# Who splits the expert weights: ScalarE and GpSimd alone, VectorE no more

## The chip, the core and the metric

The kernel runs on one core of a Trainium2 chip. Its engines are TensorE (PE, matrix products), VectorE (DVE), ScalarE (ACT), GpSimd (POOL) and SyncE (SP, which issues transfers). The metric is the device time of one launch in microseconds, the median of several runs; less is better.

## What is computed

The input is 4 sequences of 1024 rows of 256 numbers in fp32. A layer norm, an RMS norm, a projection to q, kv and a gate, a gated scan along the sequence and a residual come first. Then comes a mixture of experts, which takes most of the time:

```python
logits = x_flat @ router_w.T                      # 4096 rows, 7 experts
top_vals, top_idx = jax.lax.top_k(logits, 2)
top_w = jax.nn.softmax(top_vals, axis=-1)
g = jnp.einsum('nd,edh->enh', x_flat, wg)         # 256 -> 1024
u = jnp.einsum('nd,edh->enh', x_flat, wu)
out = jnp.einsum('enh,ehd->end', silu(g) * u, wd) # 1024 -> 256
```

The two chosen experts of a row are weighted and added, a shared expert and the residual are added too. The result is needed at fp32 accuracy.

## The kernel before

**Products in three terms.** TensorE multiplies fp32r numbers here. Each fp32 operand is split into a rounded part `hi` and a remainder `lo = value - hi`, and a product is hi\*hi + hi\*lo + lo\*hi. So each weight, each row block `xs` and each hidden block `h` has to be split before it is used.

**Slots.** The rows of the experts are worked off in slots of 256 rows: 8 slots of the shared expert (numbers 0 to 7), 38 routed slots (8 to 45, rows sorted by expert through DRAM), 8 shared slots again (46 to 53). `SA` is 8, `ROUTED` 38, `NB0` 46. A slot has 96 products for gate and up (`ps<-xs_..,w_..`, L731), in 4 pairs of 24, and 48 for down (L748), in 4 quarters of 12. TensorE may begin pair p + 2 only when VectorE has taken pair p out of PSUM (semaphore `gated`), and quarter p of down only when `h_lo` of pair p is there (`h_ready`).

**Work on a pair.** ScalarE makes `silu` (L546) from PSUM. VectorE makes `h` = PSUM \* silu (L1031). ScalarE rounds it to `h_hi` (L551). VectorE makes `h_lo` = h - h_hi (L1041), with both inputs in SBUF. Once in a slot the next rows are turned (`turn_x`, L875), rounded (`x_hi`, L490) and their remainder made (`x_lo`, L881, one input in PSUM).

**Weights.** In each routed slot a new set of weights is used, three parts of 128x2048: gate (k = 0), up (k = 1), down (k = 2). There are two buffers of `w_hi` and `w_lo`, and one `raw` for each part. SyncE loads a part into `raw` once its last remainder is made (`wlo_ready`). In slot n the set of slot n + 1 is prepared: VectorE casts gate after pair 0 and up after pair 1 (`split_hi`, L1011) and makes up's remainder in two halves after pairs 2 and 3 (`split_lo`, L1017). ScalarE casts down at the slot's end (L559). GpSimd makes the remainders of gate and down (L423, 128x2048 each, both inputs in SBUF).

**Order.** Each engine works off its own program in the order in which it is written; semaphores are the only ties between engines. An instruction that waits holds up all behind it on its engine.

Of the kernel before, what the change touches and what calls it, by code (L numbers as in the profile page):

```python
# [21 lines left out]
def preln_scan_moe_kernel(nc, x, w_qkva, gamma, router_w, w_gate, w_up, w_down,  # L22
# [12 lines left out]
    ST = SLOT // P  # L35
# [33 lines left out]
    with ExitStack() as ctx:  # L69
# [172 lines left out]
        PARTS = (2, 1, 0)  # L242
        PART_BANKS = (0, 1, 6)
        WARM = 18
        POOL_LO = (0, 2)
        NB0 = SA + ROUTED

        def place_of(j, p):
# [14 lines left out]
        def _(sp):  # L263
# [47 lines left out]
                        load_x(u, u, z_dram, u)  # L311

            def load_w(sources, m):
                for k, src in enumerate(sources):
                    sp.wait_ge(wlo_ready[k], m)
                    sp.dma_start(raw_v[k], src).then_inc(raw_in[k], 16)
# [51 lines left out]
        def _(pool):  # L368
# [72 lines left out]
            for t in range(TILES):  # L441
                for k in range(TOP):
                    pool.indirect_dma_start(  # L443
                        sorted_dram, bass.IndirectOffsetOnAxis(ap=pos[:, k, t:t + 1], axis=0),
                        z_all[:, t, :], None, bounds_check=ROUTED * SLOT - 1).then_inc(scat, 16)
            for k in POOL_LO:
                split_lo(k, 1, 1)
            with pool.Fori(0, ROUTED // 2) as i:
                for u in range(2):
                    for k in POOL_LO:  # L450
                        split_lo(k, i * 2 + (u + 2), u)


            for u in range(2):
                pool.wait_ge(y_out[u], 16 + 16 * (ROUTED // 2))
# [13 lines left out]
        def _(act):  # L469
# [70 lines left out]
            def slot(n, u, r=None, m=None, load=None, last=False, between=()):  # L540

                for p in range(PAIRS):
                    q = n * PAIRS + p
                    par = p % 2
                    act.wait_ge(gu_psum, q + 1)
                    act.activation(silu[:, par, :, :], ps[:, 2 * par:2 * par + 2, 0:SLOT], ACT.Silu  # L546
                                   ).then_inc(silu_ready, 1)
                    act.wait_ge(gated, q + 3)
                    if p == 0:
                        act.wait_ge(down_psum, n + 1)  # L550
                    act.activation(h_hi[:, 2 * p:2 * p + 2, :], h32[:, par, :, :], ACT.Copy  # L551
                                   ).then_inc(hhi_ready, 1)
                    if p in between:
                        between[p]()
                if not last:
                    x_hi(n + 1, 1 - u)
                if m is not None:
                    act.wait_ge(raw_in[2], load)
                    act.activation(w_hi[u][:, 2, :], raw[:, 2, :], ACT.Copy).then_inc(whi_ready[2], 1)  # L559
                if r is not None:  # L560
                    act.wait_ge(down_psum, n + 2)
                    act.wait_ge(y_out[u], r)
                    act.activation(y_rows[:, u, :, :], ps[:, 4:6, 0:D], ACT.Copy
                                   ).then_inc(down_free, 1)
                    act.wait_ge(down_free, n + 2)
                    act.dma_start(rows_of(y_dram, n - SA), y_rows[:, u, :, :]).then_inc(y_out[u], 16)
# [12 lines left out]
            slot(SA - 1, 1, m=1, load=32)  # L579
            with act.Fori(0, ROUTED // 2) as i:  # L580
                for u in range(2):
                    slot(i * 2 + (SA + u), u, r=i * 16 + 16, m=i * 2 + (2 + u),
                         load=i * 32 + (48 + 16 * u))
# [191 lines left out]
        def _(dve):  # L775
# [232 lines left out]
            def split_hi(k, buf, load):  # L1008

                dve.wait_ge(raw_in[k], load)  # L1010
                dve.tensor_copy(w_hi[buf][:, k, :], raw[:, k, :]).then_inc(whi_ready[k], 1)  # L1011

            def split_lo(k, m, buf, half):

                cols = slice(half * WPART // 2, (half + 1) * WPART // 2)
                dve.wait_ge(whi_ready[k], m + 1)
                ins = dve.tensor_tensor(w_lo[buf][:, k, cols], raw[:, k, cols],  # L1017
                                        w_hi[buf][:, k, cols].bitcast(F32), ALU.subtract)
                if half:
                    ins.then_inc(wlo_ready[k], 1)  # L1020

            def slot(n, u, nth, m=None, load=None, shared=None, back=None, between=()):

                for p in range(PAIRS):
                    q = n * PAIRS + p
                    par = p % 2
                    dve.wait_ge(silu_ready, q + 1)
                    dve.wait_ge(h_ready, q + 1)  # L1030
                    dve.tensor_tensor(h32[:, par, :, :], ps[:, 2 * par:2 * par + 2, SLOT:2 * SLOT],  # L1031
                                      silu[:, par, :, :], ALU.mult).then_inc(gated, 1)
                    if ("gated", p) in between:
                        between["gated", p]()
                    if m is not None and p < 2:
                        dve.wait_ge(gu_psum, n * PAIRS)
                        split_hi(p, u, load)
                    if m is not None and p >= 2:
                        split_lo(1, m, u, p - 2)
                    dve.wait_ge(hhi_ready, q + 1)  # L1040
                    dve.tensor_tensor(h_lo[:, 2 * p:2 * p + 2, :], h32[:, par, :, :],  # L1041
                                      h_hi[:, 2 * p:2 * p + 2, :].bitcast(F32), ALU.subtract
                                      ).then_inc(h_ready, 1)
# [38 lines left out]
            slot(SA - 1, 1, (R0 + 1) * LD, m=1, load=32, shared=(SA - 1) * ST)  # L1082
            with dve.Fori(0, ROUTED // 2) as i:
                for u in range(2):
                    slot(i * 2 + (SA + u), u, i * LD + LD * (R0 + 1 + u), m=i * 2 + (2 + u),
                         load=i * 32 + (48 + 16 * u))
            B0 = NB0 // 2
            dve.wait_ge(mix_ready, TOP)
            with dve.Fori(0, SBN // 2 - 1) as i:
                for u in range(2):  # L1090
# [30 lines left out]
```

## Time and profile before

| | us |
|---|---|
| three runs | 1236.89, 1237.6, 1238.63 |
| median | 1237.6 |
| span of the profiled execution, first to last instruction | 1131.8 |
| median less span | 105.8 |
| mean granted TensorE clock, share of full speed | 0.999 |

The profiled execution's whole time is not listed apart from its span, so the median stands for it; 105.8 us lie before and behind the span. The profile's page gives the busy time of each engine: PE 1057.9, VectorE 793.8, ScalarE 442.8, GpSimd 551.7 us. The timeline lists an engine's instructions with their start and duration, and in brackets how long the engine had stood idle and on whom it waited. The chain of waits follows the end of the program back to what released each step.

### The profile page before, as it was taken

The page shows a single profiled execution, that of the slowest core. Times are in us where ns is not written, and L with a number is a line of the kernel's source. Part 1 is how long each engine was busy: PE and PEld are TensorE (multiplying, and loading weights), DVE is VectorE, ACT ScalarE, POOL GpSimd, SP SyncE. Part 2 cuts the span into 40 slices and gives each one's busy share as a digit, 9 for nine tenths or more (in the row PEclk, how much of TensorE's full clock was granted, in tenths as well). Part 3 has the DMA queues.
Part 4 walks back from the last instruction along what each step waited for, and adds up shares of the span by engine and source line. Part 5 has one row for each costly group of instructions (what it writes and reads, how often), then busy time and mean ns, then how long its engine had stood idle before and what let it go on. Part 6 is the DMA issues. An engine that isn't in the chain of part 4 may idle for free.

```text
span 1131.8 us, 22368 instructions
## 1 busy us (share of the span) xinstructions
PE 1057.9 (93%) x8365; PEld 1024.8 (91%) x8365; DVE 793.8 (70%) x1088; ACT 442.8 (39%) x655; POOL 551.7 (49%) x280
## 2 busy tenths in 40 slices
PE   6999999998989898989899999999898989899998
PEld 5788999998989898989898998989898989899998
DVE  6897664466867777676868686868676777756655
ACT  3555343233343434343443434343434343432322
POOL 2234037764545463636454545555454546386450
PEclk9999999999999999999999999999999999999999
DMA  8765243325665565656565565656566566544431
GB/s 304 216 202 182 56 154 126 107 95 180 184 205 179 201 186 188 200 173 206 179 199 190 185 204 178 210 178 195 194 181 204 180 196 193 149 116 125 105 111 46
DMA packets 166622, 194.13 MB, mean 172 GB/s; under 512 B 78777, under 2 KB 152258, under 8 KB 156354
## 3 DMA queue, kind: packets, MB, share of 16 engines
q1 hardware_dynamic: 149312, 166.23, 46.9%
q0 software_dynamic: 6144, 16.79, 4.8%
q10 hardware_dynamic: 11138, 10.76, 3.0%
q8 instruction: 16, 0.26, 0.1%
q14 instruction: 12, 0.10, 0.0%
HBM read 157.03 MB, written 36.70 MB: 171 GB/s over the span
## 4 chain that ended last, share of the span: by engine, by line
PE 53%; DVE 26%; issue 17%; ACT 3%; DVEq 1%; DMA 0%; POOL 0%; POOLq 0%
PE ps L731 35%; PE ps L748 13%; DVE h_lo L1041 7%; DVE w_lo L1017 5%; DVE h L1031 4%; PE ps L650 3%; DVE w_hi L1011 3%; DVE ps L875 2%; ACT silu L546 2%; DVE y_sb L857 2%; PE ps L636 1%; DVE hT_lo L817 1%; PE ps L661 1%; DVE stats L797 0%; DMA resid<-in_L_attn_x_dram 0%
## 5 line engine op out<-in xcount | busy, mean ns | idle before, releaser
L423 POOL TENSOR_TENSOR w_lo<-raw,w_hi 128x2048 fp32r<-128x2048 f32 x81 | 388.8, 4800 | 385.3 <-ACT w_hi L559 324.7
L731 PE MATMUL ps<-xs_hi,w_hi 128*128 128x256 f32 x1728 | 489.6, 283 | 1.0 <-DVE xs_lo L881 0.8
L731 PE MATMUL ps<-xs_hi,w_lo 128*128 128x256 f32 x1728 | 489.0, 283 | 0.0
L731 PE MATMUL ps<-xs_lo,w_hi 128*128 128x256 f32 x1728 | 489.0, 283 | 0.0
L731 PEld LDWEIGHTS ps<-xs_hi,w_hi 128*128 128x128 f32 x1728 | 331.7, 192 | 1.6 <-issue 1.2
L731 PEld LDWEIGHTS ps<-xs_lo,w_hi 128*128 128x128 f32 x1728 | 331.8, 192 | 0.0
L731 PEld LDWEIGHTS ps<-xs_hi,w_lo 128*128 128x128 f32 x1728 | 331.7, 192 | 0.0
L1031 DVE TENSOR_TENSOR h<-ps,silu 128x512 f32<-128x512 f32 x216 | 147.4, 683 | 254.7 <-ACT silu L546 252.7
L748 PE MATMUL ps<-w_hi,h_hi 128*128 128x256 f32 x864 | 252.6, 292 | 56.5 <-DVE h_lo L1041 51.6
L551 ACT ACTIVATE h_hi<-h 128x512 fp32r<-128x512 f32 x216 | 136.6, 633 | 319.5 <-DVE h L1031 319.5
L748 PE MATMUL ps<-w_lo,h_hi 128*128 128x256 f32 x864 | 244.2, 283 | 0.0
L748 PE MATMUL ps<-w_hi,h_lo 128*128 128x256 f32 x864 | 244.0, 282 | 0.0
L546 ACT ACTIVATE silu<-ps 128x512 f32<-128x512 f32 x216 | 128.3, 594 | 282.5 <-PE ps L731 274.7
L748 PEld LDWEIGHTS ps<-w_hi,h_hi 128*128 128x128 f32 x864 | 165.0, 191 | 72.5 <-DVE h_lo L1041 72.5
L1011 DVE CAST w_hi<-raw 128x2048 fp32r<-128x2048 f32 x78 | 223.5, 2866 | 0.0
L1041 DVE TENSOR_TENSOR h_lo<-h,h_hi 128x512 fp32r<-128x512 f32 x216 | 147.0, 681 | 42.0 <-ACT h_hi L551 42.0
L748 PEld LDWEIGHTS ps<-w_lo,h_hi 128*128 128x128 f32 x864 | 165.3, 191 | 0.0
L748 PEld LDWEIGHTS ps<-w_hi,h_lo 128*128 128x128 f32 x864 | 165.3, 191 | 0.0
L443 POOL DMA_INDIRECT sorted_rows<-z_all,pos x64 | 66.5, 1039 | 56.2 <-issue 56.2
L1017 DVE TENSOR_TENSOR w_lo<-raw,w_hi 128x1024 fp32r<-128x1024 f32 x78 | 93.6, 1200 | 0.0
L463 POOL DMA_INDIRECT got<-expert_rows,pos x64 | 68.7, 1074 | 41.7 <-DVE resid L1004 23.3
L559 ACT ACTIVATE w_hi<-raw 128x2048 fp32r<-128x2048 f32 x39 | 74.3, 1905 | 0.0
(112 smaller groups left out, 615.3 us busy)
## 6 DMA issues: line engine op xcount, KB each, us to landing
raw<-in_L_ffn_w_gate_dram SPq DMA_DIRECT2D x38, 1024.0 KB, 4.8
raw<-in_L_ffn_w_up_dram SPq DMA_DIRECT2D x38, 1024.0 KB, 4.9
raw<-in_L_ffn_w_down_dram SPq DMA_DIRECT2D x38, 1024.0 KB, 5.6
x_rows<-sorted_rows SPq DMA_DIRECT2D x152, 64.0 KB
expert_rows<-y_rows ACTq DMA_DIRECT2D x38, 256.0 KB, 2.5
sorted_rows<-zeros SPq DMA_DIRECT2D x4, 1280.0 KB, 5.9
sorted_rows<-zeros SPq DMA_DIRECT2D x4, 1152.0 KB, 5.5
resid<-in_L_attn_x_dram SPq DMA_DIRECT2D x8, 512.0 KB, 6.8
```

What stands on the lines that cost most here:

```text
L423: pool.tensor_tensor(w_lo[buf][:, k, :], raw[:, k, :], w_hi[buf][:, k, :].bitcast(F32), ALU.subtract).then_inc(wlo_ready[k], 1)
L443: pool.indirect_dma_start(sorted_dram, bass.IndirectOffsetOnAxis(ap=pos[:, k, t:t + 1], axis=0), z_all[:, t, :], None, bounds_check=ROUTED ...
L463: pool.indirect_dma_start(got[:, r, k, :], None, y_dram, bass.IndirectOffsetOnAxis(ap=pos[:, k, t:t + 1], axis=0), bounds_check=ROUTED * S ...
L546: act.activation(silu[:, par, :, :], ps[:, 2 * par:2 * par + 2, 0:SLOT], ACT.Silu).then_inc(silu_ready, 1)
L551: act.activation(h_hi[:, 2 * p:2 * p + 2, :], h32[:, par, :, :], ACT.Copy).then_inc(hhi_ready, 1)
L559: act.activation(w_hi[u][:, 2, :], raw[:, 2, :], ACT.Copy).then_inc(whi_ready[2], 1)
L731: last = pe.matmul(o, w[:, part, at[kd]:at[kd] + P], xx[:, u, kd, :], start=i == 0, stop=i == len(terms) - 1)
L748: last = pe.matmul(ps[:, 4 + t, 0:D], hh[:, j, t * P:(t + 1) * P], w[:, 2, j * D:(j + 1) * D], start=j == 0 and i == 0, stop=j == JH - 1 a ...
L1011: dve.tensor_copy(w_hi[buf][:, k, :], raw[:, k, :]).then_inc(whi_ready[k], 1)
L1017: ins = dve.tensor_tensor(w_lo[buf][:, k, cols], raw[:, k, cols], w_hi[buf][:, k, cols].bitcast(F32), ALU.subtract)
L1031: dve.tensor_tensor(h32[:, par, :, :], ps[:, 2 * par:2 * par + 2, SLOT:2 * SLOT], silu[:, par, :, :], ALU.mult).then_inc(gated, 1)
L1041: dve.tensor_tensor(h_lo[:, 2 * p:2 * p + 2, :], h32[:, par, :, :], h_hi[:, 2 * p:2 * p + 2, :].bitcast(F32), ALU.subtract).then_inc(h_rea ...
```

## The change

VectorE casts no weights and makes no remainder of weights. ScalarE casts all three parts, each in two halves of 128x1024: in slot n the halves of down of set n + 1 behind pairs 0 and 1, and behind pair 3 up and gate of the set of slot n + 2. GpSimd makes the remainders of all three parts, in the order down, up, gate. SyncE loads in the order up, gate, down. In every slot `turn_x` moves from behind pair 2 to behind pair 1, and `x_hi` and `x_lo` move from the slot's end to behind pair 2. Slot 7 casts the whole first set and gate and up of the second; the last two routed slots are written out behind the loop.

```diff
             def load_w(sources, m):
-                for k, src in enumerate(sources):
+                for k in (1, 0, 2):
                     sp.wait_ge(wlo_ready[k], m)
-            for k in POOL_LO:
-                split_lo(k, 1, 1)
-            with pool.Fori(0, ROUTED // 2) as i:
+            for k, m in ((1, 1), (0, 1), (2, 1), (1, 2), (0, 2)):
+                split_lo(k, m, m % 2)
+            with pool.Fori(0, ROUTED // 2 - 1) as i:
                 for u in range(2):
-                    for k in POOL_LO:
-                        split_lo(k, i * 2 + (u + 2), u)
+                    split_lo(2, i * 2 + (u + 2), u)
+                    split_lo(1, i * 2 + (u + 3), 1 - u)
+                    split_lo(0, i * 2 + (u + 3), 1 - u)
...
+            def round_w(k, buf, load, half):
+                cols = slice(half * WPART // 2, (half + 1) * WPART // 2)
+                if half == 0:
+                    act.wait_ge(raw_in[k], load)
+                ins = act.activation(w_hi[buf][:, k, cols], raw[:, k, cols], ACT.Copy)
+                if half:
+                    ins.then_inc(whi_ready[k], 1)
...
+                    if p < 2 and down is not None:
+                        round_w(2, u, down, p)
+                    if p == PAIRS - 2 and not last:
+                        x_hi(n + 1, 1 - u)
...
-                if not last:
-                    x_hi(n + 1, 1 - u)
-                if m is not None:
-                    act.wait_ge(raw_in[2], load)
-                    act.activation(w_hi[u][:, 2, :], raw[:, 2, :], ACT.Copy).then_inc(whi_ready[2], 1)
+                if gate_up is not None:
+                    for k in (1, 0):
+                        for half in range(2):
+                            round_w(k, 1 - u, gate_up, half)
...
+            slot(SA - 1, 1, gate_up=48, between={0: lambda: first_weights(1), 1: lambda: first_weights(0),
+                                                 3: lambda: first_weights(2)})
...
-                    if m is not None and p < 2:
-                        dve.wait_ge(gu_psum, n * PAIRS)
-                        split_hi(p, u, load)
-                    if m is not None and p >= 2:
-                        split_lo(1, m, u, p - 2)
                     dve.wait_ge(hhi_ready, q + 1)
                     dve.tensor_tensor(h_lo[:, 2 * p:2 * p + 2, :], h32[:, par, :, :],
...
-                    if p == PAIRS - 2 and nth is not None:
+                    if p == PAIRS - 3 and nth is not None:
                         dve.wait_ge(x_split, n + 1)
                         turn_x(1 - u, nth)
-                if nth is not None:
-                    x_lo(n + 1, 1 - u)
+                    if p == PAIRS - 2 and nth is not None:
+                        x_lo(n + 1, 1 - u)
```

VectorE, one routed slot of the loop, before (`h_63` is the buffer h32, `w_hi_51` and `w_lo_52` are one of the two weight buffers):

```order
L1031 TENSOR_TENSOR h_63<-ps,silu 128x512
...
L1011 CAST w_hi_51<-raw 128x2048
L1041 TENSOR_TENSOR h_lo<-h_63,h_hi 128x512
...
L1017 TENSOR_TENSOR w_lo_52<-raw,w_hi_51 128x1024
L1041 TENSOR_TENSOR h_lo<-h_63,h_hi 128x512
...
L875 STREAM_TRANSPOSE ps<-x_rows 128x256 x2
```

and the same slot now:

```order
L1041 TENSOR_TENSOR h_63<-ps,silu 128x512
L1046 TENSOR_TENSOR h_lo<-h_63,h_hi 128x512
...
L1041 TENSOR_TENSOR h_63<-ps,silu 128x512
L1046 TENSOR_TENSOR h_lo<-h_63,h_hi 128x512
...
L899 STREAM_TRANSPOSE ps<-x_rows 128x256 x2
...
L1041 TENSOR_TENSOR h_63<-ps,silu 128x512
L1046 TENSOR_TENSOR h_lo<-h_63,h_hi 128x512
...
L905 TENSOR_TENSOR xs_lo<-ps,xs_hi 128x512
...
L1041 TENSOR_TENSOR h_63<-ps,silu 128x512
```

The weight instructions are gone from VectorE; each `h_lo` stands right behind its `h`, and `xs_lo` has moved ahead of the fourth `h`.

ScalarE, one routed slot of the loop, before:

```order
L546 ACTIVATE silu<-ps 128x512 [waits gu_psum]
L548 REGISTER_ALU
L551 ACTIVATE h_hi<-h_63 128x512 [waits gated]
L489 REGISTER_ALU
L490 ACTIVATE xs_hi<-ps 128x512 [waits xT_psum]
L558 ISA
L559 ACTIVATE w_hi_51<-raw 128x2048 [waits raw_in2]
```

and now (`w_hi_51` is the buffer of down, `w_hi_53` the other one):

```order
L548 ACTIVATE w_hi_51<-raw 128x1024 [waits raw_in2]
L557 REGISTER_ALU
L558 ACTIVATE silu<-ps 128x512 [waits gu_psum]
L560 REGISTER_ALU
L563 ACTIVATE h_hi<-h_63 128x512 [waits gated]
L548 ACTIVATE w_hi_51<-raw 128x1024
...
L563 ACTIVATE h_hi<-h_63 128x512 [waits gated]
L547 REGISTER_ALU
L548 ACTIVATE w_hi_53<-raw 128x1024 [waits raw_in1]
L548 ACTIVATE w_hi_53<-raw 128x1024
L548 ACTIVATE w_hi_53<-raw 128x1024 [waits raw_in0]
```

Six half casts stand in the slot where one whole cast stood, the second half of down behind the second `h_hi`, and four halves behind the fourth.

## Rows read from the trace of the kernel before

**Rows 1.** Head of the page: span, and an engine's busy time, share, instructions.

```profile
span 1131.8 us, 22368 instructions
...
PE 1057.9 (93%) x8365; PEld 1024.8 (91%) x8365; DVE 793.8 (70%) x1088; ACT 442.8 (39%) x655; POOL 551.7 (49%) x280
```

**Rows 2.** Chain that ended last: start us, us, what; slots 6, 8, 45, 46.

```profile
221.82 11.52 PE ps L731 x96
233.34 5.76 PE ps L748 x48
...
259.97 5.78 PE ps L731 x48
...
970.82 5.77 PE ps L731 x48
...
990.02 11.52 PE ps L731 x96
```

**Rows 3.** Timeline of VectorE in routed slot 23: start us, us, line, operation.

```profile
551.69 0.69 DVE L1031 TENSOR_TENSOR h<-ps,silu 128x512 f32<-128x512 f32 x1 [4.70 <-ACT silu L546]
552.29 1.22 DVE L1011 CAST w_hi<-raw 128x2048 fp32r<-128x2048 f32 x1
553.43 0.68 DVE L1041 TENSOR_TENSOR h_lo<-h,h_hi 128x512 fp32r<-128x512 f32 x1
554.57 0.69 DVE L1031 TENSOR_TENSOR h<-ps,silu 128x512 f32<-128x512 f32 x1 [0.46 <-ACT silu L546]
555.17 4.50 DVE L1011 CAST w_hi<-raw 128x2048 fp32r<-128x2048 f32 x1
559.60 0.68 DVE L1041 TENSOR_TENSOR h_lo<-h,h_hi 128x512 fp32r<-128x512 f32 x1
...
564.93 0.67 DVE L1041 TENSOR_TENSOR h_lo<-h,h_hi 128x512 fp32r<-128x512 f32 x1
565.53 0.67 DVE L881 TENSOR_TENSOR xs_lo<-ps,xs_hi 128x512 fp32r<-128x512 f32 x1
```

**Rows 4.** Timeline of GpSimd in the same slot.

```profile
547.70 4.62 POOL L423 TENSOR_TENSOR w_lo<-raw,w_hi 128x2048 fp32r<-128x2048 f32 x1 [8.33 <-ACT w_hi L559]
553.59 5.00 POOL L423 TENSOR_TENSOR w_lo<-raw,w_hi 128x2048 fp32r<-128x2048 f32 x1 [1.27 <-DVE w_hi L1011]
566.91 4.62 POOL L423 TENSOR_TENSOR w_lo<-raw,w_hi 128x2048 fp32r<-128x2048 f32 x1 [8.32 <-ACT w_hi L559]
```

**Rows 5.** Timeline of ScalarE in the same slot, and TensorE just before it.

```profile
546.44 0.38 PE L748 MATMUL ps<-w_hi,h_hi 128*128 128x256 f32 x1 [1.29 <-DVE h_lo L1041]
...
547.98 0.28 PE L731 MATMUL ps<-xs_hi,w_hi 128*128 128x256 f32 x1
...
551.05 0.60 ACT L546 ACTIVATE silu<-ps 128x512 f32<-128x512 f32 x1 [2.20 <-PE ps L731]
552.41 0.63 ACT L551 ACTIVATE h_hi<-h 128x512 fp32r<-128x512 f32 x1 [0.76 <-DVE h L1031]
...
563.92 0.63 ACT L551 ACTIVATE h_hi<-h 128x512 fp32r<-128x512 f32 x1 [1.89 <-DVE h L1031]
564.45 0.58 ACT L490 ACTIVATE xs_hi<-ps 128x512 fp32r<-128x512 f32 x1
564.93 1.90 ACT L559 ACTIVATE w_hi<-raw 128x2048 fp32r<-128x2048 f32 x1
```

**Rows 6.** Groups of instructions by form: count, busy us, mean ns.

```profile
L506 ACT ACTIVATE hT_hi<-ps 128x1024 fp32r<-128x1024 f32 x8 | 8.2, 1027 | 9.8 <-PE ps L617 9.8
```

**Rows 7.** Timeline of GpSimd in the first part: two instructions in a row.

```profile
79.30 4.62 POOL L423 TENSOR_TENSOR w_lo<-raw,w_hi 128x2048 fp32r<-128x2048 f32 x1
83.88 0.21 POOL L413 TENSOR_TENSOR p_var<-mv,eps 128x4 f32<-128x4 f32 x1
```

**Rows 8.** Timeline of ScalarE, first product of slot 7 taken.

```profile
243.51 0.60 ACT L546 ACTIVATE silu<-ps 128x512 f32<-128x512 f32 x1 [7.66 <-DMA sorted_rows<-z_all,pos]
```

**Rows 9.** DMA issues: count, KB each, median us from issue to landing.

```profile
raw<-in_L_ffn_w_down_dram SPq DMA_DIRECT2D x38, 1024.0 KB, 5.6
```

More of the change, by code:

```diff
@@ L244, in preln_scan_moe_kernel @@
         WARM = 18
-        POOL_LO = (0, 2)
         NB0 = SA + ROUTED
@@ L313, in load_w @@
             def load_w(sources, m):
-                for k, src in enumerate(sources):
+                for k in (1, 0, 2):
                     sp.wait_ge(wlo_ready[k], m)
-                    sp.dma_start(raw_v[k], src).then_inc(raw_in[k], 16)
+                    sp.dma_start(raw_v[k], sources[k]).then_inc(raw_in[k], 16)
             def load_expert(r, m):
@@ L445, in _ @@
                         z_all[:, t, :], None, bounds_check=ROUTED * SLOT - 1).then_inc(scat, 16)
-            for k in POOL_LO:
-                split_lo(k, 1, 1)
-            with pool.Fori(0, ROUTED // 2) as i:
+            for k, m in ((1, 1), (0, 1), (2, 1), (1, 2), (0, 2)):
+                split_lo(k, m, m % 2)
+            with pool.Fori(0, ROUTED // 2 - 1) as i:
                 for u in range(2):
-                    for k in POOL_LO:
-                        split_lo(k, i * 2 + (u + 2), u)
+                    split_lo(2, i * 2 + (u + 2), u)
+                    split_lo(1, i * 2 + (u + 3), 1 - u)
+                    split_lo(0, i * 2 + (u + 3), 1 - u)
+            split_lo(2, ROUTED, 0)
+            split_lo(1, ROUTED + 1, 1)
+            split_lo(0, ROUTED + 1, 1)
+            split_lo(2, ROUTED + 1, 1)
             for u in range(2):
@@ L538, in _, with slot @@
                                    ).then_inc(whi_ready[g - 4], 1)
-            def slot(n, u, r=None, m=None, load=None, last=False, between=()):
+            def round_w(k, buf, load, half):
[5 more added lines that the diff above has]
+                    ins.then_inc(whi_ready[k], 1)
+            def slot(n, u, r=None, down=None, gate_up=None, last=False, between=()):
                 for p in range(PAIRS):
@@ L578, in _, with first_weights @@
             act.wait_ge(scat, 16 * TOP * TILES)
-            slot(SA - 1, 1, m=1, load=32)
-            with act.Fori(0, ROUTED // 2) as i:
-                for u in range(2):
-                    slot(i * 2 + (SA + u), u, r=i * 16 + 16, m=i * 2 + (2 + u),
-                         load=i * 32 + (48 + 16 * u))
+            def first_weights(k):
+                for half in range(2):
+                    round_w(k, 1, 32, half)
+            slot(SA - 1, 1, gate_up=48, between={0: lambda: first_weights(1), 1: lambda: first_weights(0),
+                                                 3: lambda: first_weights(2)})
+            with act.Fori(0, ROUTED // 2 - 1) as i:
+                for u in range(2):
+                    slot(i * 2 + (SA + u), u, r=i * 16 + 16, down=i * 32 + (48 + 16 * u),
+                         gate_up=i * 32 + (64 + 16 * u))
+            y_last = 16 * (ROUTED // 2)
+            slot(NB0 - 2, 0, r=y_last, down=16 * (ROUTED + 1), gate_up=16 * (ROUTED + 2))
+            slot(NB0 - 1, 1, r=y_last, down=16 * (ROUTED + 2))
             with act.Fori(0, SBN // 2 - 1) as i:
@@ L1006, in mix, with slot @@
                                                  op0=ALU.mult, op1=ALU.add).then_inc(mixed, 1)
[L1008 to L1022, printed above, removed]
+            def slot(n, u, nth, shared=None, back=None, between=()):
                 for p in range(PAIRS):
@@ L1081, in _ @@
             dve.wait_ge(scat, 16 * TOP * TILES)
-            slot(SA - 1, 1, (R0 + 1) * LD, m=1, load=32, shared=(SA - 1) * ST)
-            with dve.Fori(0, ROUTED // 2) as i:
+            slot(SA - 1, 1, (R0 + 1) * LD, shared=(SA - 1) * ST)
+            with dve.Fori(0, ROUTED // 2 - 1) as i:
                 for u in range(2):
-                    slot(i * 2 + (SA + u), u, i * LD + LD * (R0 + 1 + u), m=i * 2 + (2 + u),
-                         load=i * 32 + (48 + 16 * u))
+                    slot(i * 2 + (SA + u), u, i * LD + LD * (R0 + 1 + u))
             B0 = NB0 // 2
+            slot(NB0 - 2, 0, LD * B0)
+            slot(NB0 - 1, 1, LD * (B0 + 1))
             dve.wait_ge(mix_ready, TOP)
```

## The prediction, made before the changed kernel was run

> **What bounds the kernel now.** I read the chain that ended last first. It is a row of TensorE's products: a shared slot takes 11.52 + 5.76 = 17.28 us without a gap [rows 2]. The 38 routed slots begin at 259.97 and end at 990.02, which is 730.05 / 38 = 19.21 us each [rows 2]. So TensorE stands still for 1.93 us in each, 73.3 us in all, and that is the most that this change can win there. The second view is the timeline of one routed slot, the one whose first product starts at 547.98 [rows 5]. TensorE stood 1.29 us before the last quarter of down and waited for `h_lo` [rows 5]. Why `h_lo` was late is in VectorE's rows: the cast of up took 4.50 us where the cast of gate took 1.22 [rows 3]. GpSimd made a remainder from 553.59 to 558.59 [rows 4]. The cast asked for its turn at 555.17, inside that stretch, and ended 1.08 us after it. So the cast was kept out until GpSimd was done. VectorE's `h`, with one input in PSUM, started at 554.57 inside the same stretch and took 0.69, as elsewhere: it isn't kept out.
>
> Following VectorE from the slot's start (S) checks this reading. `h` of pair 0 at S + 3.71, cast to 5.53, remainder from 5.61 to 10.61, second cast ends at 11.69; then come `h_lo`, `h`, half a remainder, `h_lo`, the turn, `h`, half a remainder and the last `h_lo`, which ends at S + 17.62 (565.60), and the last quarter, 1.54 us from its first product to the next slot's [rows 5]. That gives 19.2.
>
> **What goes.** VectorE loses two casts and two half remainders in each slot, the 3.3 us of waiting (4.50 - 1.22) with them. If nothing came in their place, VectorE would have 4 `h`, 4 `h_lo`, a turn and an `xs_lo`, at 0.67 to 0.69 each [rows 3] about 7 us of work in 17.28.
>
> **What comes.** GpSimd has three remainders a slot instead of two: 3 x 4.62 = 13.9 us [rows 4], and back to back 4.58 apart [rows 7]. That alone fits in 17.28. ScalarE has six half casts instead of one whole one. A half isn't in the trace. Half of the whole cast is 0.95 [rows 5], and an instruction of the same width from PSUM takes 1.03 [rows 6]; I take 1.03, which holds the fixed cost too, and 0.93 to the next start. Six are 6.2 us, 4.3 more than before. ScalarE was busy for 442.8 of the span's 1131.8 us [rows 1], so it has the room. Order decides, not load.
>
> **The term that decides: `h_lo` under a remainder.** Before, no `h_lo` starts while GpSimd makes a remainder; VectorE's order and the data kept them apart but for one overlap. In each routed slot `h_lo` (553.43 to 554.11) still runs when gate's remainder is started at 553.59, and that remainder takes 5.00, while the other one, with no `h_lo` beside it, takes 4.62 [rows 3, 4]. (The one at 547.70 had an `h` beside it at 551.69 and stayed at 4.62, so it isn't `h` that costs.) The 0.38 us fit a remainder that waits until `h_lo` has finished reading, for the two overlap by 0.52. Now GpSimd is busy for 13.9 us of a slot and `h_lo` must start inside. The bounds: 0.68 us as ever [rows 3], or waiting for the remainder's end, as the cast did. I take the second: the nearest row is the 5.00, which has these same two operations excluding each other the other way round. By the cast, an instruction kept out ends 1.08 behind the remainder where it takes 1.22 alone, so `h_lo` ends 0.68 - 0.14 = 0.54 behind it, and VectorE's next starts 0.46 behind it (0.07 to 0.08 before its predecessor's end, as at 559.60).
>
> The Trainium skill has the rule, in "SBUF — State Buffer", section "Who interferes with whom": a VectorE instruction with two inputs in SBUF contends with a GpSimd instruction that reads SBUF, one with at most one SBUF input outside the two-port modes doesn't, and whoever comes second waits for the whole of the first. No row here shows `h_lo` as the second; the 5.00 shows it as the first, and agrees. By this rule the time is the forecast below, without it the first rival.
>
> **The loop that results.** Follow one turn from the end of down's remainder (0). The `h_lo` of pair 2 has waited for it. `xs_lo` starts at 0.46, `h` of pair 3 at 1.06 (0.60 apart, [rows 3]), `h_hi` at 1.78 (0.72 behind `h`, [rows 3, 5]), up's first half cast at 2.31 (0.53 behind, [rows 5]), the second at 3.24, done at 4.27. Up's remainder starts at 4.35 (0.08 behind, as 566.83 to 566.91), gate's at 8.93, and ends at 13.55. Meanwhile `h_lo` of pair 3 was free and ended at about 3.13, the last quarter follows (0.05 + 1.54), and the next slot starts at 4.72. There `h_lo` of pair 0 could start 5.1 us in (553.04 + 0.04 against 547.98), at 9.8: 0.9 us after gate's remainder has begun. So it waits until 13.55. `h` of pair 1, which stands behind it on VectorE, starts at 14.01, `h_hi` at 14.73, down's second half cast at 15.26, done at 16.29; `h_lo` of pair 1 and the turn find GpSimd idle. Down's remainder runs from 16.37 to 20.99 and catches `h_lo` of pair 2 again. The turn takes **20.99 us**: three remainders and 7.2 us of handing over between the three engines, with TensorE's 17.28 inside it. Loads don't stand in it: raw of down is free at 0, lands near 5.8 (5.6 from its issue, [rows 9]) and is wanted at 9.7; up and gate have more.
>
> **The sum.** Slots 9 to 45: 37 x (20.99 - 19.21) = +65.9. Slot 7: ScalarE may start at 243.51 as before [rows 8], casts two whole parts between its pairs, and `h_lo` of pair 1 (ready at about 249.3) meets up's remainder, 247.4 to 252.0. If it gets in behind that one, slot 8 starts at about 261.8, if gate's goes first at 264.0, against 259.97: +1.8 to +4.0, I take +3. Slot 8: its ScalarE waits before `silu` of pair 1 for down's raw of the second set, which is free only when down's first remainder ends (about 265 to 268) and lands 5.8 later; worked through, the slot takes 23.6 to 25.6 against 19.21: I take +5.4. Slots 0 to 6 and those from 46 on have no remainders of a next set beside them and stay as they are; that `turn_x` and `xs_lo` come earlier there costs nothing, since VectorE stands idle before each `h`. The gathers behind the routed slots wait for the last stored rows in both kernels. Sum 65.9 + 3 + 5.4 = +74.3. The sum is made on a span of 1131.8 [rows 1], whose 105.8 around it don't change, so the median 1237.6 becomes **1312**.
>
> **Rivals.** (1) `h_lo` isn't kept out. Then nothing holds TensorE: per slot `h_lo` of pair 3 ends near 14.4 and is wanted at 15.8, GpSimd needs 13.9 of 17.28. 38 x 1.93 = -73.3; slot 7 ends some 2 earlier, slot 8 costs 3.8 for the first loads: 1237.6 - 73.3 - 2.0 + 3.8 = **1166**. For it: no row shows a waiting `h_lo`. Against it: the 5.00. It decides whether the rest holds. (2) `h_lo` of pair 0 slips in between up's and gate's remainder, or shares with GpSimd in part. It would have to come 0.9 us sooner than I worked out, or up's remainder begin as much later. Then three remainders run nearly without a break: 13.9, two `h_lo` let in (1.0), and from `h_lo` of pair 2 to up's next remainder 4.35: about 19.2 a slot, with the first two slots **1245**, up to 1290 for what lies between. Against it: the 0.9 comes out of the loop itself and holds in each turn. (3) Remainders are slower beside more traffic: at 5.00 for each, 3 x 0.38 x 37 = +42, so **1354**. The 5.00 came from an `h_lo` at the start, and in the loop only pair 1's comes near one (it ends 0.3 us before down's remainder starts), so one of three at most: +14.
>
> **How the numbers follow.** The loop as worked out has 0.75; its own range is 1300 to 1335 (half casts of 0.95 take off 7, a pushed remainder adds 14, the first slots 3 either way, some more for handing over). Rival 1 has 0.14, rival 2 0.10, rival 3 0.01. The range reaches from 1238 to 1350: it leaves out rival 1 and little else. About 0.2% is what a measurement can tell here. Faster: rival 1 and a little of 2, 0.15; within 0.2%: 0.02; slower 0.83.
>
> **What would show it.** In the changed kernel's timeline a routed slot should take 21.0; `h_lo` of pairs 0 and 2 should be listed with about 4.3 and 3.3 us and end 0.54 behind a remainder; those of pairs 1 and 3 with 0.68. TensorE should wait for `gated` before pair 3 and for `h_lo` in quarters 2 and 3. Remainders stay at 4.62 and half casts near 1.03. If all `h_lo` have 0.68 inside remainders and slots take 17.28, rival 1 was right. If GpSimd has no gap ahead of down's remainder, it is rival 2. If ScalarE's waits name the loads of raw, the handing over was mis-sized.

## The result, and the profile after

The changed kernel takes 1309.08 us (four runs, 1308.96 to 1310.95) where the kernel before takes 1237.86 (1236.89 to 1238.63): the ratio is 1.0579, with a 95% interval of 1.0564 to 1.0594. It is slower by 71.2 us; 74.3 were forecast.

The head of the page, an engine's busy time, its share of the span and its instructions:

```profile
span 1307.2 us, 22325 instructions
...
PE 1092.5 (84%) x8365; PEld 1044.7 (80%) x8365; DVE 746.2 (57%) x932; ACT 582.0 (45%) x850; POOL 714.1 (55%) x319
```

Against [rows 1], VectorE has 156 instructions less and still only 47.6 us less busy time. The page's groups (count, busy us, mean ns; then the idle time before them) say why:

```profile
L422 POOL TENSOR_TENSOR w_lo<-raw,w_hi 128x2048 fp32r<-128x2048 f32 x120 | 554.6, 4639 | 364.3 <-ACT w_hi L548 356.0
...
L1046 DVE TENSOR_TENSOR h_lo<-h,h_hi 128x512 fp32r<-128x512 f32 x216 | 392.1, 1815 | 152.5 <-ACT h_hi L563 144.5
...
L548 ACT ACTIVATE w_hi<-raw 128x1024 fp32r<-128x1024 f32 x234 | 233.0, 1044 | 4.7 <-DMA raw<-in_L_ffn_w_down_dram 4.7
```

The mean `h_lo` takes 1815 ns, against 0.67 to 0.68 us in [rows 3]. A routed slot of the loop on VectorE (start us, us, line, operation; in brackets the idle time before and whom it waited for):

```profile
386.32 0.69 DVE L1041 TENSOR_TENSOR h<-ps,silu 128x512 f32<-128x512 f32 x1 [5.30 <-ACT silu L558]
387.79 4.25 DVE L1046 TENSOR_TENSOR h_lo<-h,h_hi 128x512 fp32r<-128x512 f32 x1 [0.78 <-ACT h_hi L563]
391.96 0.68 DVE L1041 TENSOR_TENSOR h<-ps,silu 128x512 f32<-128x512 f32 x1
393.34 0.69 DVE L1046 TENSOR_TENSOR h_lo<-h,h_hi 128x512 fp32r<-128x512 f32 x1 [0.70 <-ACT h_hi L563]
...
394.77 0.69 DVE L1041 TENSOR_TENSOR h<-ps,silu 128x512 f32<-128x512 f32 x1
396.16 3.34 DVE L1046 TENSOR_TENSOR h_lo<-h,h_hi 128x512 fp32r<-128x512 f32 x1 [0.70 <-ACT h_hi L563]
399.42 0.68 DVE L905 TENSOR_TENSOR xs_lo<-ps,xs_hi 128x512 fp32r<-128x512 f32 x1
400.02 0.68 DVE L1041 TENSOR_TENSOR h<-ps,silu 128x512 f32<-128x512 f32 x1
401.40 0.69 DVE L1046 TENSOR_TENSOR h_lo<-h,h_hi 128x512 fp32r<-128x512 f32 x1 [0.70 <-ACT h_hi L563]
```

and on GpSimd over the same time (x2 is two remainders without a gap), the counterpart of [rows 4]:

```profile
382.26 9.23 POOL L422 TENSOR_TENSOR w_lo<-raw,w_hi 128x2048 fp32r<-128x2048 f32 x2 [4.39 <-ACT w_hi L548]
394.33 4.62 POOL L422 TENSOR_TENSOR w_lo<-raw,w_hi 128x2048 fp32r<-128x2048 f32 x1 [2.85 <-ACT w_hi L548]
403.34 9.22 POOL L422 TENSOR_TENSOR w_lo<-raw,w_hi 128x2048 fp32r<-128x2048 f32 x2 [4.38 <-ACT w_hi L548]
```

The two remainders end at 391.49 and the `h_lo` listed from 387.79 on ends at 392.04, 0.55 behind. Down's remainder ends at 398.95 and the `h_lo` listed from 396.16 on ends at 399.50, 0.55 behind again. The `h` of pairs 0 and 2 (386.32 and 394.77), which have an input in PSUM, start inside remainders and take 0.69, so they are not held up. (`xs_lo` and the `h` of pairs 1 and 3 start while GpSimd stands idle and say nothing on this.) One turn of GpSimd is 403.34 - 382.26 = 21.08 us. Between its pieces it waits 4.39 and 2.85 us for ScalarE's casts. TensorE's first products of slots 9 and 46 stand at:

```profile
361.68 0.28 PE L755 MATMUL ps<-xs_hi,w_hi 128*128 128x256 f32 x1
...
1141.16 0.28 PE L755 MATMUL ps<-xs_hi,w_hi 128*128 128x256 f32 x1
```

That is 779.48 / 37 = 21.07 us a slot, against 19.21 in [rows 2]. TensorE's waits in the loop (from 370 to 1120 us: us in total, times, longest) are the two that were foreseen:

```profile
PE ps L772 <- DVE h_lo L1046: 62.8, 72, 0.9
...
PE ps L755 <- DVE h L1041: 46.1, 36, 1.3
```

They are two waits for `h_lo` and one for `h` (the semaphore `gated`) in each of 36 slots: 108.9 / 36 = 3.0 us. The distance from TensorE's own 17.28 is 3.8 us. The other 0.8 lie around the three waits, some 0.26 at each: the two products on either side of a wait that is listed with 0.84 start at 377.36 and 378.48, and the one behind them at 378.70, which is 1.34 us where two starts of 0.12 would be 0.24.

**What doesn't fit.** Slots 7 to 45 explain 73.9 us (slots 7 and 8 take 45.30 here and 40.08 before, the rest is 779.48 - 37 x 19.21 = 68.7), but the span is 175.4 us longer than the profiled one of before. The table of stretches (busy us and count of each engine, granted clock, DMA share, GB/s) shows where the rest lies:

```profile
120.00:167.00 47.00, 46.84 (x389) 46.48 (x388) 32.00 (x69) 18.98 (x32) 8.10 (x10) 1.00 0.27 88
167.00:250.00 83.00, 20.19 (x61) 15.32 (x62) 2.08 (x3) 1.23 (x2) 55.44 (x57) 0.53 0.32 109
250.00:316.00 66.00, 66.00 (x550) 66.00 (x549) 29.42 (x47) 22.91 (x37) 0.00 (x0) 1.00 0.05 12
...
1158.00:1181.00 23.00, 12.13 (x51) 10.62 (x50) 3.29 (x7) 0.60 (x1) 15.33 (x15) 0.59 0.44 125
...
190.00:210.00 20.00, 2.92 (x8) 2.00 (x7) 0.00 (x0) 0.00 (x0) 15.43 (x16) 0.50 0.30 105
```

From 167 to 250 us TensorE starts 61 products where it started 389 in the 47 us before; VectorE starts three instructions, ScalarE two. GpSimd goes on issuing its scatters of rows, 1.28 us apart. Nothing that the profile shows is waited for:

```profile
186.42 0.37 PE L772 MATMUL ps<-w_lo,h_hi 128*128 128x256 f32 x1 [1.74 <-issue]
187.83 0.37 PE L772 MATMUL ps<-w_hi,h_lo 128*128 128x256 f32 x1 [1.03 <-issue]
```

A second, shorter stretch of this kind lies at 1158 to 1181, while GpSimd issues gathers. Whether these stretches belong to the change is the first question of the experiments.

### The profile page after: what moved, and what is told of

It reads as the page before. It is cut to its first block, busy times and chain, and to the rows that moved or that the text cites. A ratio compares the mean times of both kernels' runs of the same rounds, so it can differ in the third digit from the quotient of the medians.

```text
span 1307.2 us, 22325 instructions
## 1 busy us (share of the span) xinstructions
PE 1092.5 (84%) x8365; PEld 1044.7 (80%) x8365; DVE 746.2 (57%) x932; ACT 582.0 (45%) x850; POOL 714.1 (55%) x319
## 4 chain that ended last, share of the span: by engine, by line
PE 36%; issue 31%; DVE 17%; ACT 14%; DMA 1%; POOL 1%; another core or an unknown queue 0%; DVEq 0%; ACTq 0%; POOLq 0%
PE ps L755 22%; PE ps L772 10%; DVE h L1041 8%; ACT h_hi L563 7%; ACT silu L558 3%; ACT w_hi L548 3%; DVE h_lo L1046 3%; PE ps L674 3%; DVE xs_lo L905 2%; DVE y_sb L881 1%; PE ps L660 1%; DVE hT_lo L841 1%; PE ps L685 1%; DVE stats L821 0%
## 5 line engine op out<-in xcount | busy, mean ns | idle before, releaser
L422 POOL TENSOR_TENSOR w_lo<-raw,w_hi 128x2048 fp32r<-128x2048 f32 x120 | 554.6, 4639 | 364.3 <-ACT w_hi L548 356.0
L755 PE MATMUL ps<-xs_hi,w_hi 128*128 128x256 f32 x1728 | 497.7, 288 | 63.5 <-DVE h L1041 51.4
L1046 DVE TENSOR_TENSOR h_lo<-h,h_hi 128x512 fp32r<-128x512 f32 x216 | 392.1, 1815 | 152.5 <-ACT h_hi L563 144.5
L755 PEld LDWEIGHTS ps<-xs_hi,w_hi 128*128 128x128 f32 x1728 | 335.3, 194 | 71.6 <-DVE h L1041 59.3
L755 PEld LDWEIGHTS ps<-xs_hi,w_lo 128*128 128x128 f32 x1728 | 335.2, 194 | 14.0 <-issue 14.0
L548 ACT ACTIVATE w_hi<-raw 128x1024 fp32r<-128x1024 f32 x234 | 233.0, 1044 | 4.7 <-DMA raw<-in_L_ffn_w_down_dram 4.7
L466 POOL DMA_INDIRECT got<-expert_rows,pos x64 | 68.6, 1072 | 75.8 <-DVE resid L1028 49.0
L1065 DVE TENSOR_TENSOR resid<-ps,resid 128x512 f32 (+1 forms) x16 | 11.0, 690 | 89.4 <-remote 74.0
L674 PE MATMUL ps<-hT_hi,wT_hi 128*128 128x512 f32 x96 | 39.6, 412 | 3.2 <-DVE hT_lo L841 3.2
```

The lines of the kernel that those rows point to most:

```text
L466: pool.indirect_dma_start(got[:, r, k, :], None, y_dram, bass.IndirectOffsetOnAxis(ap=pos[:, k, t:t + 1], axis=0), bounds_check=ROUTED * S ...
L548: ins = act.activation(w_hi[buf][:, k, cols], raw[:, k, cols], ACT.Copy)
L674: last = pe.matmul(ps[:, bank + e, :], w[:, part, kd, at:at + P], h[:, c, kd, :], start=i == 0, stop=i == len(terms) - 1)
L755: last = pe.matmul(o, w[:, part, at[kd]:at[kd] + P], xx[:, u, kd, :], start=i == 0, stop=i == len(terms) - 1)
```

## The experiments

Each run of an experiment is compared with runs of the kernel before on the same chip. They ran on two further chips. On neither of them is the stretch there that was just shown. That it is in the runs on the first chip is the one thing needed to read the numbers: 1309 there is 1209 here, 1238 there is 1135 here.

**1. The kernel before again.** No edit. The theory is that `h_lo` waits under GpSimd's remainders and that the stretch has nothing to do with the change. The rival is that the stretch is part of what the change costs. This run asks what lies around the span of an ordinary execution of the kernel before.

> The kernel before, unchanged, to see where the 105.8 us between its profiled span (1131.8) and its time (1237.6) lie. Theory A, as the prediction had it: they lie before and behind the span; then the spans of its timed runs are near 1132 too. Theory B: the timed executions hold a stretch like the one that the changed kernel's trace shows (TensorE standing for 'issue' between 167 and 247 us and again from 1150 to 1196, about 100 us in all, while GpSimd issues its scatters and gathers), and the profiled execution of before had none; then the spans of its timed runs are near 1236 and a new profile may show the stretch.

Measured: 1134.83 us beside 1134.87 for the same kernel, ratio 0.9998 (0.9988 to 1.0008). The profiled execution took 1134.86 with a span of 1133.1: only 1.8 us lie around the span, as they do in the changed kernel's (1309.0 and 1307.2). So the statement that 105.8 us lie around the span was wrong. The profiled execution that the forecast rested on was one without the stretch, and the runs of 1237.6 must have had 103 us inside their spans. This last step is a conclusion from the times: no trace of such a run of the kernel before is on record.

**2. The changed kernel again.** No edit.

> The changed kernel, unchanged, beside the kernel before on one chip. Theory A (routed slots of 21.07 against 19.21 us make the loss): on a chip without the stretch in which the engines crawl while GpSimd issues its scatters, kernel before at 1134.9 and this one at 1134.9 + 73.8 = 1208.7, ratio 1.065. On a chip with the stretch, some 1238 and 1309 as in the first measurement, ratio 1.058. Theory C (the stretch of the changed kernel's trace is its own, made by its order): this one stays near 1309 while the kernel before takes 1135, ratio 1.15.

Measured: 1208.87 (1208.09 to 1209.6) where the kernel before takes 1134.75, ratio 1.0654 (1.0636 to 1.0672). That is +74.1 us. The window from 190 to 210, last in the table above, in this trace:

```profile
190.00:210.00 20.00, 20.00 (x169) 20.00 (x168) 8.21 (x13) 6.00 (x10) 15.33 (x16) 1.00 0.34 112
```

TensorE starts 169 products beside the same scatters, where it started 8, and the clock is at 1.00 instead of 0.50. Slots 7, 9 and 46 start here at:

```profile
240.06 0.28 PE L755 MATMUL ps<-xs_hi,w_hi 128*128 128x256 f32 x1
...
285.50 0.28 PE L755 MATMUL ps<-xs_hi,w_hi 128*128 128x256 f32 x1
...
285.66 2.89 PE ps L755 x24
...
1065.02 11.52 PE ps L755 x96
```

(The last two rows are from the chain: start, length, what. It lists a slot's start 0.16 behind the timeline, slot 9 at 285.66.) Slots 9 to 45 take 1065.02 - 285.66 = 779.4 us, as in the first trace. The stretch has moved slot 9 by 361.68 - 285.50 = 76.2 us and the end by another 24.2; together they are the 100.4 us between the two spans. The stretch belongs to the chip or its state at the time, not to the change.

**3. `h` in PSUM.** One edit on the changed kernel: from slot 2 on, `h` is written to a free bank of PSUM, so `h_lo` reads one input from PSUM and one from SBUF; ScalarE reads `h` for `h_hi` from there too. The bank holds one pair, so `h` of a pair waits for the `h_lo` of the pair before.

```diff
+        def h_buf(n, par):
+            if isinstance(n, int) and n < 2:
+                return h32[:, par, :, :]
+            return ps[:, 7, :].rearrange("p (a n) -> p a n", a=2)
...
-                    dve.wait_ge(h_ready, q + 1)
+                    dve.wait_ge(h_ready, q + (1 if isinstance(n, int) and n < 2 else 2))
...
-                    dve.tensor_tensor(h_lo[:, 2 * p:2 * p + 2, :], h32[:, par, :, :],
+                    dve.tensor_tensor(h_lo[:, 2 * p:2 * p + 2, :], h_buf(n, par),
```

> The changed kernel with h kept in bank 7 of PSUM from slot 2 on, so that h_lo has one input in SBUF and one in PSUM; nothing else moves. Theory 1 (a VectorE instruction with two SBUF inputs is kept out for the whole of a GpSimd remainder): all h_lo take about 0.68 us, also inside remainders, routed slots fall from 21.07 to TensorE's 17.28, slots 9 to 45 win 37 x 3.79 = 140 us and slots 7 and 8 some 3 to 6: about 1309 - 145 = 1164 us. Theory 2 (h_lo is late for another reason: ScalarE's casts and the order of handing over): no change beyond 1%, 1300 to 1320 us.

Measured: 1061.88 us (1061.38 to 1063.13) where the kernel before takes 1134.87, ratio 0.9356 (0.9341 to 0.9372). This is 147 us less than the changed kernel takes without the stretch; 145 less were expected (the 1164 holds on the first chip's scale, 100 us higher). VectorE and GpSimd in a slot of the loop:

```profile
560.38 0.70 DVE L1046 TENSOR_TENSOR ps<-ps,silu 128x512 f32<-128x512 f32 x1 [6.48 <-ACT silu L563]
561.75 0.69 DVE L1051 TENSOR_TENSOR h_lo<-ps,h_hi 128x512 fp32r<-128x512 f32 x1 [0.67 <-ACT h_hi L568]
...
567.52 0.69 DVE L1051 TENSOR_TENSOR h_lo<-ps,h_hi 128x512 fp32r<-128x512 f32 x1 [0.67 <-ACT h_hi L568]
...
555.15 9.23 POOL L427 TENSOR_TENSOR w_lo<-raw,w_hi 128x2048 fp32r<-128x2048 f32 x2 [2.08 <-ACT w_hi L553]
565.63 4.64 POOL L427 TENSOR_TENSOR w_lo<-raw,w_hi 128x2048 fp32r<-128x2048 f32 x1 [1.25 <-ACT w_hi L553]
```

`h_lo` starts at 561.75 and at 567.52, both inside remainders (555.15 to 564.38, 565.63 to 570.27), and takes 0.69 both times. The routed slots go down to 17.28, TensorE's own time. Engines, order, weights, casts and remainders are those of the changed kernel. What differs is where `h` lies, and of the instructions that touch it only `h_lo` had been long: `h` took 0.69 before, and 0.70 here. That shows the cause directly.

**4. `h` in PSUM in the kernel before.** The same edit on the other kernel.

> The kernel before with h kept in bank 7 of PSUM from slot 2 on. Theory 1: the remainder of gate, pushed by the h_lo at its start, falls from 5.00 to 4.62 us and the cast behind it ends 0.38 earlier, a routed slot takes 18.83 instead of 19.21: 38 x 0.38 = 14 us less, about 1223 us; the cast keeps its 4.1 to 4.5 us, since it is the cast's own two ports that are refused. Theory 2: 5.00 stays and the time stays within 0.3% of 1237.9.

Measured: 1126.36 (1125.65 to 1126.59), ratio 0.9924 (0.9908 to 0.9941), that is -8.5 us where -14 were expected. The remainder that took 5.00 in [rows 4], and the cast behind it:

```profile
569.61 4.62 POOL L428 TENSOR_TENSOR w_lo<-raw,w_hi 128x2048 fp32r<-128x2048 f32 x1 [1.39 <-DVE w_hi L1016]
...
571.20 4.13 DVE L1016 CAST w_hi<-raw 128x2048 fp32r<-128x2048 f32 x1
```

The remainder is at 4.62 and the cast has lost the same 0.37: the 5.00 was indeed a remainder that waited for an `h_lo`, the row on which the forecast had leaned. It also bounds what PSUM alone is worth: without the move of the weights to ScalarE the cast is still kept out for 2.9 us a slot, and the slot takes 19.04. Two gaps make up 0.19 of the missing 0.2 us a slot. An `h` that comes right behind an `h_lo` starts 0.71 behind its start instead of 0.60, since with a single bank it has to wait for its end. And the first `h` of a slot starts 0.72 behind its `silu` (586.02 and 586.74), where it is 0.64 in [rows 3, 5]; why was not looked into.

So the slots give 38 x 0.17 = 6.5 of the 8.5 us. Another 1.6 come from slot 7 (19.26 us against 20.87), and this the forecast had not seen. In the kernel before ScalarE waits there for the last scatter and starts 4.57 us into the slot (243.51 against 238.94). Here it starts 3.14 in and waits for TensorE alone, for the scatters end sooner: from the second to the last it is 79.2 us here and 83.1 in both traces of the kernel before. The rows of the kernel before show what stretches them:

```profile
232.52 0.69 DVE L1041 TENSOR_TENSOR h_lo<-h,h_hi 128x512 fp32r<-128x512 f32 x1 [0.70 <-ACT h_hi L551]
232.76 1.30 POOL L443 DMA_INDIRECT sorted_rows<-z_all,pos  x1 [0.30 <-issue]
234.37 0.97 POOL L443 DMA_INDIRECT sorted_rows<-z_all,pos  x1 [0.30 <-issue]
```

Of the 64 scatters, 16 begin while an `h_lo` runs: 12 of them take 1.22 to 1.32 us, the other four 0.98 to 1.01. The 47 that begin at other times take 0.97 or 0.98 (the first is left out: it takes 1.25 in every run). With `h` in PSUM ten begin under an `h_lo`, and each takes 0.97 or 0.98.

**5. Half remainders.** The changed kernel, with each remainder on GpSimd made in two instructions. The amount of work is the same and so is its order.

```diff
-                pool.tensor_tensor(w_lo[buf][:, k, :], raw[:, k, :], w_hi[buf][:, k, :].bitcast(F32),
-                                   ALU.subtract).then_inc(wlo_ready[k], 1)
+                for half in range(2):
+                    cols = slice(half * WPART // 2, (half + 1) * WPART // 2)
+                    ins = pool.tensor_tensor(w_lo[buf][:, k, cols], raw[:, k, cols],
+                                             w_hi[buf][:, k, cols].bitcast(F32), ALU.subtract)
+                ins.then_inc(wlo_ready[k], 1)
```

> The changed kernel with each remainder of 128x2048 on GpSimd as two instructions of 128x1024 (2.3 us each). Theory A (an h_lo waits for the end of the one GpSimd instruction that is under way, and VectorE gets in between two): no h_lo over 2.8 us, TensorE covers what is left, routed slots at TensorE's 17.28 us, 37 x (17.28 - 21.07) = -140 us: about 1067 where the kernel before takes 1135, ratio 0.94. Rival B (GpSimd's second half goes on first, since it waits for nothing): h_lo at 4.3 and 3.3 us as in the changed kernel, slots near 21.1, 1209 us, ratio 1.065. Rival C (the short instructions cost more than their share, 2.6 us or over): GpSimd needs 15.6 us or more of a slot, an h_lo waits up to 3 us, slots at 17.3 to 18, 1067 to 1095.

Measured: 1065.39 (1065.16 to 1067.03) where the kernel before takes 1134.75, ratio 0.9388 (0.9372 to 0.9404), 143.5 us less than the changed kernel on the same chip. One slot on VectorE, then on GpSimd:

```profile
565.55 1.11 DVE L1049 TENSOR_TENSOR h_lo<-h,h_hi 128x512 fp32r<-128x512 f32 x1 [0.70 <-ACT h_hi L566]
...
568.43 1.05 DVE L1049 TENSOR_TENSOR h_lo<-h,h_hi 128x512 fp32r<-128x512 f32 x1 [0.70 <-ACT h_hi L566]
...
571.45 0.94 DVE L1049 TENSOR_TENSOR h_lo<-h,h_hi 128x512 fp32r<-128x512 f32 x1 [0.70 <-ACT h_hi L566]
...
558.96 9.96 POOL L424 TENSOR_TENSOR w_lo<-raw,w_hi 128x1024 fp32r<-128x1024 f32 x4 [1.56 <-ACT w_hi L551]
569.42 5.24 POOL L424 TENSOR_TENSOR w_lo<-raw,w_hi 128x1024 fp32r<-128x1024 f32 x2 [0.50 <-ACT w_hi L551]
```

`h_lo` gets in between two halves that stand back to back: the two here take 1.11 and 1.05 while four halves run from 558.96 to 568.92, and those four need 9.96 instead of the 9.23 for the same columns. So rival B, that GpSimd's waiting instruction goes first, is wrong. Rival C is half right: a half costs 2557 ns in the mean, 0.25 more than half of 4.62, so GpSimd works 15.2 us of each slot, but it still fits and the slots are at 17.28. This run tells two readings of the forecast apart that `h` in PSUM doesn't: the wait is for the one instruction under way, not for GpSimd to run out of work, and shorter instructions shorten it.

**6. The moved row step undone.** The changed kernel with `turn_x` behind pair 2 again and `x_hi`, `x_lo` at the slot's end. In the loop this puts `turn_x` (0.69) in place of `xs_lo` (0.60) ahead of the `h` of pair 3, and `x_hi` ahead of ScalarE's four half casts. Both lie in the handing over.

```diff
-                    if p == PAIRS - 3 and nth is not None:
+                    if p == PAIRS - 2 and nth is not None:
                         dve.wait_ge(x_split, n + 1)
                         turn_x(1 - u, nth)
-                    if p == PAIRS - 2 and nth is not None:
-                        x_lo(n + 1, 1 - u)
+                if nth is not None:
+                    x_lo(n + 1, 1 - u)
...
-                    if p == PAIRS - 2 and not last:
-                        x_hi(n + 1, 1 - u)
...
+                if not last:
+                    x_hi(n + 1, 1 - u)
```

> The changed kernel with one part undone: turn_x again behind pair 2, x_hi and x_lo again at the slot's end. By the loop of the prediction: the turn (0.69) stands in for xs_lo (0.60) between the waiting h_lo of pair 2 and h of pair 3, and x_hi (0.48 to the next start) stands ahead of up's casts: 0.57 more in each slot, 21.64, in all +21 us: about 1330. If the loop isn't what bounds the slot, this costs nothing: 1309.

Measured: 1229.79 (1229.3 to 1230.21) where the kernel before takes 1134.87, ratio 1.0839 (1.0821 to 1.0857). In its chain (start us, us, what) the same 24 products of every second slot stand at:

```profile
589.22 2.89 PE ps L755 x24
632.39 2.90 PE ps L755 x24
675.58 2.89 PE ps L755 x24
```

That is 43.17 and 43.19 for two slots, 21.59 for one, against 21.07. The moved row step saves the changed kernel 0.52 us a slot, 19 us in slots 9 to 45 and 20.9 in the whole (1229.79 - 1208.87).

**7. The moved row step alone.** The mirror of 6: the kernel before with that step moved and nothing else.

> The kernel before with the moved row step alone: the turn behind pair 1, x_hi and x_lo behind pair 2, VectorE's casts and remainders as before. Theory A (VectorE's row behind up's cast is the tight place, so 0.60 us put ahead of the fourth h is paid by every slot): slot 19.21 + 0.6 = 19.8, 37 x 0.6 = +22 us, 1157 where the kernel before takes 1135. Rival B (xs_lo at the slot's end was on the path and goes off it, as it does in the changed kernel, where the order was worth 0.52 us a slot): slot 18.7, -19 us, 1116.

Measured: 1156.83 (1155.94 to 1156.93) where the kernel before takes 1134.75, ratio 1.0192 (1.0175 to 1.0209), +22.1 us. The chain lists slots 8, 9 and 46 at:

```profile
260.44 5.78 PE ps L731 x48
...
280.25 5.77 PE ps L731 x48
...
1013.28 11.52 PE ps L731 x96
```

The 38 routed slots take 752.84 / 38 = 19.81 us each.

So the same edit costs 0.6 us a slot in one kernel and saves 0.52 in the other. In the kernel before VectorE runs without a break behind up's cast, so what is put ahead of the fourth `h` delays the last `h_lo`. In the changed one the tight place is the handing over from VectorE to ScalarE to GpSimd.

| kernel | kernel before, same chip | us | ratio | routed slot |
|---|---|---|---|---|
| before | 1134.87 | 1134.83 | 0.9998 | 19.21 |
| changed | 1134.75 | 1208.87 | 1.0654 | 21.06 |
| changed, `h` in PSUM | 1134.87 | 1061.88 | 0.9356 | 17.28 |
| before, `h` in PSUM | 1134.87 | 1126.36 | 0.9924 | 19.04 |
| changed, half remainders | 1134.75 | 1065.39 | 0.9388 | 17.28 |
| changed, row step undone | 1134.87 | 1229.79 | 1.0839 | 21.59 |
| before, row step moved | 1134.75 | 1156.83 | 1.0192 | 19.81 |

Against the kernel before, the change and `h` in PSUM together win 73.0 us; `h` in PSUM alone wins 8.5 and the change alone loses 74.1. One conflict turns a gain into the loss. Three versions of the table beat both kernels. The changed kernel with `h` in PSUM is the fastest by its median, but it and the half remainders ran on different chips and their intervals touch at 0.9372.

## Why the prediction was right, and where it was not

**The deciding term: right.** `h_lo` is kept out until the remainder ends. It was taken from a row in which the roles were reversed (5.00 against 4.62 in [rows 4]) and from the cast that had waited (4.50 in [rows 3]). Forecast were about 4.3 and 3.3 us for pairs 0 and 2, ending 0.54 behind; measured 4.25 and 3.34 in the slot shown (pair 0 has 4.24 to 4.33 in the loop), ending 0.55 behind. Pairs 1 and 3 take 0.69. This is what the Trainium skill, "SBUF — State Buffer", section "Who interferes with whom", states for a VectorE instruction with two inputs in SBUF that comes second. The trace of after now shows it, and the `h_lo` with a PSUM input (0.69 inside remainders, experiment 3) shows the other half of that rule.

**The loop: right.** Worked out 20.99 us, measured 21.07. The handing over is 4.39 + 2.85 = 7.24 on GpSimd, against 7.2. The small rest is the half cast, 1.04 to 1.05 instead of 1.03, and two remainders in a row, 9.23 instead of 9.20. Loads are not on the path of the loop, and remainders stay at 4.62. The sum for slots 9 to 45 was +65.9. It is 779.48 - 710.77 (37 x 19.21) = +68.7 in the first trace and 779.36 - 710.77 = +68.6 in the one without the stretch.

**The first two slots: too high, mostly by choice of the middle.** Forecast were +3 for slot 7 and +5.4 for slot 8. By the trace without the stretch (experiment 2), slot 7 starts at 240.06, slot 8 at 261.82 and slot 9 at 285.50. Slot 7 takes 21.76 against 259.97 less 239.10 (233.34 + 5.76) in [rows 2], which is 20.87: +0.9. Slot 8 takes 23.68 against 19.21: +4.5. The rows behind slot 7's term, from the first trace:

```profile
323.66 9.61 POOL L422 TENSOR_TENSOR w_lo<-raw,w_hi 128x2048 fp32r<-128x2048 f32 x2 [84.17 <-ACT w_hi L548]
...
325.48 3.37 DVE L1046 TENSOR_TENSOR h_lo<-h,h_hi 128x512 fp32r<-128x512 f32 x1 [0.70 <-ACT h_hi L563]
```

Two remainders in a row take 9.61 here where they take 9.23 in the loop, and `h_lo` ends at 328.85, between them. The forecast left open who goes first and took a middle; VectorE does, which was its lower branch of +1.8, and gate's remainder waits 0.38. Experiment 5 shows the same in every slot. That slot 7 costs even less than +1.8 has another reason. The forecast counted from ScalarE's first `silu`, which waits for the scatters: slot 8 starts 261.82 - 243.36 = 18.46 us behind it, in the kernel before 259.81 - 243.51 = 16.30 (in the timeline's starts), +2.2. But slot 7's first product came 1.12 us later in this trace while the scatters ended 0.15 sooner. The wait of slot 8's ScalarE for down's raw is there as forecast (experiment 2's chain):

```profile
266.16 5.72 DMA raw<-in_L_ffn_w_down_dram
```

In all +68.6 + 0.9 + 4.5 = 74.0, and experiment 2 measured 74.1, against 74.3. That the total is so close is luck: the loop's +2.7 and the first slots' -3.0 cancel.

**The 105.8 us "before and behind the span": wrong.** Around the span lie 1.8 us. By the times, the rest was inside the spans of the executions that were timed, as the stretch during the scatters and gathers, which the profiled execution did not have. The record doesn't say whether that one ran on the same chip. The forecast's total held because both kernels are longer by nearly the same on the first chip: 1237.86 - 1134.8 = 103.1 us before and 1309.08 - 1208.87 = 100.2 after. That this excess is about 3 us smaller in the changed kernel is the difference between 71.2 measured and 74.1 without it. The step that failed is the sentence that called the difference of two executions something that lies around one of them; had the change touched the scatters, it would have mattered.

**The rivals.** No exclusion (1166): wrong as a description of this kernel. Its arithmetic, all slots at 17.28, is what `h` in PSUM gives: -73.0 us against the kernel before on the same chip, where 1237.6 - 1166 = 71.6 were worked out. (Not all slots are at 17.28 there: slot 8 takes 280.11 - 257.53 = 22.58, 5.3 more, where 3.8 had been allowed for.) The `h_lo` of pair 0 slipping in between two remainders: not in the loop, since it comes 0.9 us after the second has begun, as worked out (remainders from 382.26 and about 386.9, `h_lo` at 387.79). Remainders at 5.00: no, 4639 ns in the mean.

## What to carry to other kernels

Before moving elementwise work from VectorE to GpSimd, list VectorE's instructions that will run beside it with both inputs in SBUF: each can be held up until the GpSimd instruction under way ends. Here one row in which the other party was held up, and one of a cast that had waited, were enough to forecast it. Then put one of the two inputs in PSUM or cut GpSimd's instructions short; here either turned +74 us into -73 and -69. And if the median of the timed runs and the span of the profiled execution lie 106 us apart, ask first whether the profiled one is an execution like the others.

## What the runs showed of the hardware

**An engine's instructions can crawl beside GpSimd's indirect transfers.** On the first chip TensorE, VectorE and ScalarE nearly stopped from about 167 to 247 us and for some 20 us at the gathers. The 64 scatters were issued from 157 to 239.5, so the stretch began 10 us behind the first and outlasted the last by some 8. In it TensorE started 61 products in 83 us, where it starts one per 0.12 us at full pace, with no releaser named. The mean granted clock was 0.53 and 0.59 in the two stretches, and together they cost 100 us. GpSimd kept its pace of 1.28 us per scatter. On two other chips the kernel before, and on one of them the changed one, ran through the same scatters at full pace (169 products in 20 us, clock 1.00). TensorE's clock was at 1.00 (2.4 GHz) in the 47 us before and at 0.50 (1.2 GHz) from 190 to 210, when TensorE was nearly idle. Whether the low clock only follows the idleness was not told apart. What starves the engines wasn't tried, as no chip of the experiments showed it. It stays open, and so does whether it goes with the chip or with its state.

**VectorE goes in between two GpSimd instructions that stand back to back** when it already waits, and pushes the second one by 0.38 us (9.61 against 9.23).

**A VectorE instruction with both inputs in SBUF also lengthens a scatter that GpSimd begins under it**, by some 0.32 us (1.22 to 1.32 instead of 0.97, 12 of 16 in the kernel before); with one input in PSUM it does not (none of 10, experiment 4).

**Two instructions of 128x1024 on GpSimd cost more than one of 128x2048** while VectorE's `h_lo` contend: 2557 ns each, against 4639. How much of the 0.25 us is a fixed cost and how much the pushes of four `h_lo` a slot wasn't measured apart: by an estimate from the push above, four of 0.38 would be 1.5 us a slot, and GpSimd's 15.20 less 13.85 (three at about 4.62) is 1.35, so the pushes alone could account for it.
